# Splitting the first loads of a gated cross-attention kernel: first weight quarter on ScalarE's queue and cast by VectorE, first 400 rows of x in two pieces of 200, 24 warm-up matmuls for 31

## What is computed

```python
memory_proj = einsum('bme,de->bmd', memory, W_mem)
scores = einsum('bnd,bmd->bnm', hidden, memory_proj) / sqrt(D)
attn = softmax(scores, axis=-1)
memory_context = einsum('bnm,bmd->bnd', attn, memory_proj)
gate_input = concatenate([hidden, memory_context], axis=-1)
gate = sigmoid(einsum('bnf,df->bnd', gate_input, W_gate) + b_gate)
out = rmsnorm(hidden + gate * memory_context) * norm_w
```

## Time and profile before

| what | value |
| --- | --- |
| median of 3 runs | 294.86 us (294.81 to 295.05) |
| the profiled execution's own time | 294.93 us |
| its span, first to last instruction | 293.1 us |
| TensorE busy | 285.1 us, 97% of the span |
| VectorE busy | 175.7 us, 60% |
| ScalarE busy | 158.9 us, 54% |
| transfers | 52.19 MB, 178 GB/s over the span |

### The profile page before, as it was taken

The page is one execution under the profiler, slowest core; times in us unless marked ns, Lnnn a source line. Parts: engine busy times, 40 slices in busy tenths (PEclk is TensorE's granted clock), DMA queues, the critical chain, the costliest instruction groups (busy, mean ns, idle before and its releaser), DMA issues.

```text
span 293.1 us, 4177 instructions
## 1 busy us (share of the span) xinstructions
PE 285.1 (97%) x1671; PEld 273.7 (93%) x1671; DVE 175.7 (60%) x252; ACT 158.9 (54%) x235; POOL 4.2 (1%) x10
## 2 busy tenths in 40 slices
PE   8999999999999999999999999999999999999991
PEld 7999999898998989899898998999999999999990
DVE  2757664568656585865758562374347765476755
ACT  4648254555494645748355454435545964556632
POOL 2000000000000000000000000000000000010000
PEclk9999999999999999999999999999999999999998
DMA  6999280692948849296692411229806511623333
GB/s 209 398 401 286 101 319 0 172 351 71 323 146 217 306 121 340 76 290 229 164 358 93 127 20 58 72 72 384 180 31 225 168 48 63 134 83 94 119 131 143
DMA packets 32851, 52.19 MB, mean 178 GB/s; under 512 B 11280, under 2 KB 16144, under 8 KB 32832
## 3 DMA queue, kind: packets, MB, share of 16 engines
q1 hardware_dynamic: 32832, 51.92, 54.8%
HBM read 47.33 MB, written 4.33 MB: 176 GB/s over the span
## 4 chain that ended last, share of the span: by engine, by line
PE 92%; issue 4%; DMA 1%; ACT 1%; DVE 1%; SPq 0%; POOLq 0%; POOL 0%; ACTq 0%
PE ps L375 66%; PE ps L469 11%; PE ps L492 9%; PE ps L483 1%; DMA w_stage<-w_mem 1%; PE ps L496 1%; PE ps L503 1%; DVE acc L987 0%; DVE square_sum L964 0%; ACT gate_square L782 0%; PE ps L415 0%; PE ps L410 0%; PE ps L412 0%; POOLq L56 0%; POOL rms_late L1109 0%
## 5 line engine op out<-in xcount | busy, mean ns | idle before, releaser
L375 PE MATMUL ps<-act_hi,w_turn_hi 128*128 128x400 f32 (+2 forms) x216 | 60.4, 342 | 0.0
L375 PE MATMUL ps<-act_hi,w_turn_lo 128*128 128x400 f32 (+2 forms) x216 | 59.7, 339 | 0.0
L375 PE MATMUL ps<-act_lo,w_turn_hi 128*128 128x400 f32 (+2 forms) x216 | 59.7, 339 | 0.0
L375 PEld LDWEIGHTS ps<-act_hi,w_turn_hi 128*128 128x128 f32 x216 | 39.4, 188 | 0.9
L375 PEld LDWEIGHTS ps<-act_hi,w_turn_lo 128*128 128x128 f32 x216 | 40.0, 188 | 0.0
L375 PEld LDWEIGHTS ps<-act_lo,w_turn_hi 128*128 128x128 f32 x216 | 40.0, 188 | 0.1
L813 DVE TENSOR_TENSOR w_turn_lo<-w_stage,w_turn_hi 128x1024 fp32r<-128x1024 f32 (+2 forms) x20 | 22.3, 1116 | 24.5 <-ACT w_turn_hi L609 23.0
L813 DVE TENSOR_TENSOR cn_lo<-cn_stage,cn_hi 128x1536 fp32r<-128x1536 f32 (+1 forms) x16 | 23.7, 1484 | 5.6 <-ACT cn_hi L628 5.6
L813 DVE TENSOR_TENSOR ct_lo<-ct_stage,ct_hi 128x1444 fp32r<-128x1444 f32 x16 | 25.8, 1653 | 0.5 <-ACT ct_hi L620 0.5
L696 ACT ACTIVATE pc<-ps,row_inv 100x512 f32<-100x512 f32 x8 | 5.5, 688 | 31.5 <-PE ps L496 31.5
L609 ACT ACTIVATE w_turn_hi<-w_stage 128x1024 fp32r<-128x1024 f32 x17 | 17.9, 1053 | 7.6 <-PE ps L375 5.9
(11 more groups left out here) (147 smaller groups left out, 570.5 us busy)
## 6 DMA issues: line engine op xcount, KB each, us to landing
ct_stage<-ctxT SPq DMA_DIRECT2D x16, 722.0 KB, 8.2
cn_stage<-ctxN SPq DMA_DIRECT2D x8, 768.0 KB, 6.0
cn_stage<-ctxN SPq DMA_DIRECT2D x8, 512.0 KB, 4.1
w_stage<-w_gate_x SPq DMA_DIRECT2D x8, 512.0 KB, 6.1
w_stage<-w_gate_mc SPq DMA_DIRECT2D x8, 512.0 KB, 3.5
x_again<-xT SPq DMA_DIRECT2D x1, 2688.0 KB, 10.3
cn_stage<-ctxN SPq DMA_DIRECT2D x8, 320.0 KB
acc<-xT SPq DMA_DIRECT2D x6, 400.0 KB, 7.5
```

The lines of the kernel that those rows point to most:

```text
L375: done = nc.tensor.matmul(o, wgt, stream[h][part], start=first and wgt is wh and part == 0, stop=last and wgt is wl, skip_group_check=onto)
```

## The change

SyncE's first three transfers are now the two pieces of 200 rows of x and the second weight quarter. The first weight quarter is issued by ScalarE, as the first thing in its program, and cast by VectorE, as the first thing in VectorE's. TensorE does the six matmuls of c = 0 and 1 as twelve with 200 columns, six for each piece of x; those of c = 2 and 3 are as before. The number of warm-up matmuls goes from 31 to 24. The matmuls into the shared banks carry a flag that changes what the build tracks, not what they do.

```diff
-WARM_UP = 31
+WARM_UP = 24
...
-            sp.dma_start(acc[:, 0, 0:H], xT[0:P, 0:H]).then_inc(x_first_in, 16)
             for i in range(2):
-                cols = slice(i * C // 2, (i + 1) * C // 2)
-                sp.dma_start(w_stage[:, 0, cols], w_mem[0][:, cols]).then_inc(w_first_in[i], 16)
+                rows = slice(i * H // 2, (i + 1) * H // 2)
+                sp.dma_start(acc[:, 0, rows], xT[0:P, rows]).then_inc(x_first_in[i], 16)
+            sp.dma_start(w_stage[:, 0, C // 2:C], w_mem[0][:, C // 2:C]).then_inc(w_first_in[1], 16)
             sp.dma_start(acc[:, 0, H:R], xT[0:P, H:R]).then_inc(x_in[0], 16)
...
+                    (xh, xl) = early[0]
+                    pe.wait_ge(quarter_hi_done, 1)
+                    pe.wait_ge(first_hi_done, 1)
+                    for c, (wh, _) in pairs[0:2]:
+                        nc.tensor.matmul(left(c, 0), wh, xh, start=True, stop=False, skip_group_check=True)
+                    pe.wait_ge(first_lo_done, 1)
+                    for c, (wh, _) in pairs[0:2]:
+                        nc.tensor.matmul(left(c, 0), wh, xl, start=False, stop=False, skip_group_check=True)
+                    pe.wait_ge(first_lo_done, 2)
+                    for c, (_, wl) in pairs[0:2]:
+                        nc.tensor.matmul(left(c, 0), wl, xh, start=False, stop=False, skip_group_check=True)
...
-            act.wait_ge(x_first_in, 16)
-            nc.scalar.activation(act_hi[:, 0, 0:H], acc[:, 0, 0:H], ACT.Copy).then_inc(first_hi_done, 1)
+            act.dma_start(w_stage[:, 0, 0:C // 2], w_mem[0][:, 0:C // 2]).then_inc(w_first_in[0], 16)
             for i in range(2):
-                cols = slice(i * C // 2, (i + 1) * C // 2)
-                act.wait_ge(w_first_in[i], 16)
-                nc.scalar.activation(w_hi[0][:, cols], w_stage[:, 0, cols], ACT.Copy).then_inc(first_hi_done, 1)
+                rows = slice(i * H // 2, (i + 1) * H // 2)
+                act.wait_ge(x_first_in[i], 16)
+                nc.scalar.activation(act_hi[:, 0, rows], acc[:, 0, rows], ACT.Copy).then_inc(first_hi_done, 1)
+            act.wait_ge(w_first_in[1], 16)
+            nc.scalar.activation(w_hi[0][:, C // 2:C], w_stage[:, 0, C // 2:C], ACT.Copy).then_inc(first_hi_done, 1)
...
+            dve.wait_ge(w_first_in[0], 16)
+            nc.vector.tensor_copy(w_hi[0][:, 0:quarter], w_stage[:, 0, 0:quarter]).then_inc(quarter_hi_done, 1)
             dve.wait_ge(first_hi_done, 1)
-            minus(act_lo[:, 0, 0:H], acc[:, 0, 0:H], act_hi[:, 0, 0:H]).then_inc(first_lo_done, 1)
+            minus(act_lo[:, 0, 0:half], acc[:, 0, 0:half], act_hi[:, 0, 0:half]).then_inc(first_lo_done, 1)
```

More of the change, by code:

```diff
@@ L171, in build @@
         x_second_in, second_hi_done, second_lo_done = sem("x_second_in"), sem("second_hi_done"), sem("second_lo_done")
-        x_first_in, w_first_in = sem("x_first_in"), [sem(f"w_first_in{i}") for i in range(2)]
+        x_first_in, w_first_in = [sem(f"x_first_in{i}") for i in range(2)], [sem(f"w_first_in{i}") for i in range(2)]
+        quarter_hi_done = sem("quarter_hi_done")
         w_in = [sem(f"w_in{s}") for s in range(2)]
@@ L395, in _ @@
                 if k == 0:
[L396 to L406, removed]
+                    pairs = [(c, w_tile(0, c)) for c in range(KC)]
@@ new lines, in _, with left @@
+                    early = [(act_hi[:, 0, a:a + H // 2], act_lo[:, 0, a:a + H // 2]) for a in (0, H // 2)]
+                    def left(c, i):
+                        return bank(c, H // 2, P, i * H // 2)
+                    (xh, xl) = early[0]
[3 more added lines that the diff above has]
+                        nc.tensor.matmul(left(c, 0), wh, xh, start=True, stop=False, skip_group_check=True)
@@ new lines, in _ @@
+                    pe.wait_ge(first_lo_done, 1)
[4 more added lines that the diff above has]
+                        nc.tensor.matmul(left(c, 0), wl, xh, start=False, stop=False, skip_group_check=True)
+                    (xh, xl) = early[1]
+                    pe.wait_ge(first_hi_done, 2)
@@ new lines, in _ @@
+                    for c, (wh, _) in pairs[0:2]:
+                        nc.tensor.matmul(left(c, 1), wh, xh, start=False, stop=False, skip_group_check=True)
+                    for c, (_, wl) in pairs[0:2]:
+                        nc.tensor.matmul(left(c, 1), wl, xh, start=False, stop=False, skip_group_check=True)
+                    pe.wait_ge(first_lo_done, 3)
+                    for c, (wh, _) in pairs[0:2]:
+                        nc.tensor.matmul(left(c, 1), wh, xl, start=False, stop=False, skip_group_check=True)
@@ new lines, in _ @@
+                    (xh, xl) = halves(act_hi, act_lo, 0)[0]
+                    pe.wait_ge(first_hi_done, 3)
+                    for c, (wh, _) in pairs[2:KC]:
+                        nc.tensor.matmul(bank(c, H), wh, xh, start=True, stop=False, skip_group_check=True)
+                    for c, (wh, _) in pairs[2:KC]:
+                        nc.tensor.matmul(bank(c, H), wh, xl, start=False, stop=False, skip_group_check=True)
+                    pe.wait_ge(first_lo_done, 4)
+                    for c, (_, wl) in pairs[2:KC]:
+                        nc.tensor.matmul(bank(c, H), wl, xh, start=False, stop=False, skip_group_check=True)
@@ L409, in _ @@
                     for c, (wh, _) in pairs:
-                        nc.tensor.matmul(bank(c + 4, H), wh, xh, start=True, stop=False)
+                        nc.tensor.matmul(bank(c + 4, H), wh, xh, start=True, stop=False, skip_group_check=True)
                     for c, (_, wl) in pairs:
-                        nc.tensor.matmul(bank(c + 4, H), wl, xh, start=False, stop=False)
+                        nc.tensor.matmul(bank(c + 4, H), wl, xh, start=False, stop=False, skip_group_check=True)
                     pe.wait_ge(x_lo_done, 1)
                     for c, (wh, _) in pairs:
-                        nc.tensor.matmul(bank(c + 4, H), wh, xl, start=False, stop=False)
+                        nc.tensor.matmul(bank(c + 4, H), wh, xl, start=False, stop=False, skip_group_check=True)
                     continue
@@ L420, in _ @@
                     for c in range(KC):
-                        three([bank(c, H)], w_tile(0, KC + c), halves(act_hi, act_lo, 1)[:1], False, False)
+                        three([bank(c, H)], w_tile(0, KC + c), halves(act_hi, act_lo, 1)[:1], False, False, onto=True)
                     pe.wait_ge(x_lo_done, 2)
                     for c in range(KC):
-                        done = three([bank(c + 4, H)], w_tile(0, KC + c), halves(act_hi, act_lo, 1)[1:], False, False)
+                        done = three([bank(c + 4, H)], w_tile(0, KC + c), halves(act_hi, act_lo, 1)[1:], False, False,
+                                     onto=True)
                     done.then_inc(w_used, 1)
@@ L432, in _ @@
                         done = three([bank(c, H), bank(c + 4, H)], w_tile(k // 2 % 2, k % 2 * 4 + c),
-                                     halves(act_hi, act_lo, k), False, False)
+                                     halves(act_hi, act_lo, k), False, False, onto=True)
                 else:
@@ L437, in _ @@
                             done = three([bank(c + 4 * h, H)], w_tile(k // 2 % 2, k % 2 * 4 + c),
-                                         halves(act_hi, act_lo, k)[h:h + 1], False, True)
+                                         halves(act_hi, act_lo, k)[h:h + 1], False, True, onto=True)
                             if (h, c) != (1, KC - 1):
@@ L839, in split_ctx @@
                                                    ALU.subtract).then_inc(cn_lo_done, 1)
+            half, quarter = H // 2, C // 2
+            dve.wait_ge(w_first_in[0], 16)
+            nc.vector.tensor_copy(w_hi[0][:, 0:quarter], w_stage[:, 0, 0:quarter]).then_inc(quarter_hi_done, 1)
             dve.wait_ge(first_hi_done, 1)
-            minus(act_lo[:, 0, 0:H], acc[:, 0, 0:H], act_hi[:, 0, 0:H]).then_inc(first_lo_done, 1)
[L843 to L846, removed]
+            minus(act_lo[:, 0, 0:half], acc[:, 0, 0:half], act_hi[:, 0, 0:half]).then_inc(first_lo_done, 1)
+            dve.wait_ge(quarter_hi_done, 1)
+            minus(w_lo[0][:, 0:quarter], w_stage[:, 0, 0:quarter], w_hi[0][:, 0:quarter]).then_inc(first_lo_done, 1)
+            dve.wait_ge(first_hi_done, 2)
+            minus(act_lo[:, 0, half:H], acc[:, 0, half:H], act_hi[:, 0, half:H]).then_inc(first_lo_done, 1)
+            dve.wait_ge(first_hi_done, 3)
+            minus(w_lo[0][:, quarter:C], w_stage[:, 0, quarter:C], w_hi[0][:, quarter:C]).then_inc(first_lo_done, 1)
             dve.wait_ge(x_hi_done, 1)
```

## The result

The change measured 296.31 us in the median of 22 runs, against 294.81 us for the kernel before (22 runs, 294.35 to 295.68). The ratio is 1.0034, with a 95% interval of 1.0018 to 1.0051: it is slower, by a third of a per cent. The forecast was 294.7, within 294.2 to 295.5.

A forecast was written before the change was run, and what follows sets the result against it. TensorE, busy 97% of the span, bounds the kernel; the second weight quarter's landing decides the start. Its -0.14 us, other terms 0.0, takes 294.93 to 294.79, less 0.07 to the runs' median: 294.7 us, range 294.2 to 295.5.

The forecast's parts named there:

- the late clock: Slower rival at the kernel's start: with 24 warm-up matmuls TensorE's clock rises after the 6.1 us restart; 295.6 us, chance 0.15.
- The price: Cost of a late clock rise: nothing ahead of the 6.1 us restart, half the time until the rise after; 295.6 us.
- The first matmul: Start of TensorE's real work: first weight quarter and first piece of x arrive earlier, start 3.5 to 3.75 instead of 4.17.
- The second quarter: Transfer of the second weight quarter, on the chain at the start: lands 0.14 us earlier, the deciding term.
- The cap: If the second quarter alone came earlier, gain stops at 0.37 us, TensorE then waiting at x's right half and k = 2.
- the sum: Terms at the start together: first piece, small matmuls and warm-up 0.0 each, second quarter -0.14, from 294.93 to 294.79 us.
- The small matmuls and the table load: Before the second quarter: twelve matmuls done by 5.2, at most 5.8, and ScalarE's table load ending near 2.45; both hidden, 0.0.

The follow-up runs named there:

- the filled one: The change with 24 warm-up matmuls plus two bfloat16 matmuls behind each of the first five pairs of small matmuls; 297.17 us median, ratio 1.0056.

## Why the prediction was wrong

**The step that failed is the chance and the price of the late clock.** The mechanism was named, with its place: warm-up ending at 3.3, rise seen somewhere behind it. It was given 0.15; the change had 13 late runs of 21, and six of eight when run again. The argument against it was that "TensorE has work or warm-up for most of 0.76 to 5.2 even now". The runs show that this is no argument: with work added among the small matmuls 7 of 12 were still late, and every late profile shows TensorE at work without a break from 3.9 us on. What goes with the late runs is the length of the warm-up, here told by how far it reaches, with its starts 0.107 us apart from 0.76: to 1.6 us (8 matmuls) 4 of 4 are late; to 3.3 (24) 19 of 29 in the change, the one of 731.98 left out, and 10 of 12 in the kernel before; to 3.76 (28) 2 of 12; to 4.07 or beyond (31, 38, or 10 of 400 columns) 0 of 69 in six kernels. With a longer warm-up a hole did no harm: not one of 0.48 us inside a warm-up that reaches 4.1 (0 of 11), and not one as long in front of the first real matmul, from 4.07 to 4.55, where only the first quarter was moved (0 of 12; in its profile the full clock is on record from 4.39, inside the hole). And real matmuls that begin at 3.9 did not make up for what the warm-up lacked.

**The price.** I wrote that what is slow ahead of the second quarter is free and that behind it half of the time is lost, and said 295.6. Measured 296.57. Two terms were too small. The small matmuls were let off with "even 2.2 us from 3.6 on ends at 5.8"; at the low clock they take 0.213 us each and end at 6.60, 0.82 us behind the release. And the rise came near 9, not near the 7.6 that 295.6 amounts to.

**The first matmul.** Predicted 3.5 to 3.75, measured 3.91. The cast is 0.29 us, inside 0.21 to 0.42, but the first quarter took 2.8 us to land from ScalarE's queue, not 2.4: VectorE began at 3.56 instead of 3.1. That x's pieces on the other queue slowed it is likely and not shown. The first piece of x was late too: its cast began at 3.39, and I had written no later than 3.28. As said, it costs nothing in an early execution. The rule of the Trainium skill ("DMA: Bandwidth & Descriptors", section "Issuing engines are not separate DMA queues") agrees: the issue was 0.45 us earlier, and the landing was not (0.72 + 2.8 = 3.5 us, before 1.18 + 2.4 = 3.6).

**The second quarter.** Predicted 0.14 us sooner, measured 0.35 in the profiled execution, but the same order as before gave 0.45 in another (3.55 us against 4.00). The landing moves by itself between executions, so no part of it can be put down to the change. I had taken it for regular, from three close run times. The cap does not explain that they were close: the execution with 3.55 us kept its 0.45 us through k = 2.

**The cap.** Said to be 0.37 us behind the second quarter, with no wait at k = 2. TensorE came 0.35 ahead into k = 1 and was held 0.19 us at k = 2, since the low part of the slot was itself ready 0.22 us later (VectorE's subtraction began at 12.27, before at 12.05), which left room for 0.15. This room is no constant: in the kernel before with 24 the subtraction began at 11.80, and nothing waited. So the 0.15 us that is left of the lead comes from a landing 0.35 us sooner and a wait that was not forecast; that it is so near the 0.14 of the sum is luck.

**The small matmuls and the table load** were hidden in the early execution as said: the last small one ended at 5.68 (predicted 5.2), ahead of the 5.78 at which the next began, and the table load at 2.44 (predicted 2.45). But TensorE was to stand idle there for longer than the 0.59 us of before, and it was 0.10 us: the first matmul came later than predicted and the second quarter sooner.

**The lower group** sits at 294.77 us, against a forecast of 294.7 and a median before of 294.81. With the clock up in time, the change does nothing that can be told.

## What to carry to other kernels

An edit that shortens a warm-up changes a chance, not a duration: keep it as long as it can be hidden, and read many run times before reading any profile, because the one profiled execution can be of the good kind (here 294.84 us, below the 294.93 of the one profiled before). Price work at the start of a kernel at the lower clock as well, since what a wait hides at one level may stick out at the other. And where a stream of loads comes close behind, starting sooner gains only up to the next wait, here 0.15 us of 0.35 in one execution, and all of 0.45 in another whose loads came sooner too.

## What the runs showed of the hardware that was not expected

- The rise of the clock falls into two ranges. Each trace records from when on the full clock was granted (the column in the windows prints 1.00 ahead of that as well), and the starts of the matmuls bear this out. In ten traces this is at 3.9 to 6.6 us: 3.92 in the kernel before, 3.95 and 4.03 in the two early executions with 24, 4.35 to 6.62 in seven others, all with warm-ups that reach 4.07 us or more. In the four late ones (28, 24, 8 and the filled one) it is at 8.86 to 9.87, although TensorE worked from 3.9 on in all of them; there is none between. With 24, no rise was seen between 4.03 and 8.86, just where five of the longer warm-ups have theirs (5.27 to 6.62). This suggests that a short warm-up loses those executions whose clock would have risen there. No run shows it.
- The page "TensorE: Matmul & The Clock Gate" of the Trainium skill, section "What you observe", has the rise some 4 us into sustained matmuls, moving by half a microsecond. The early range lies around that, but is wider: 3.2 to 5.9 us behind the first matmul. The late one, 8.1 to 9.1 us behind it, is not near it where the warm-up and the real matmuls are taken as one run of work. No run here shows what makes one execution late and another not with the same program, and why five microseconds of unbroken matmuls did not bring the clock up sooner is left open.
- A transfer of 128 KB in the same place of the same queue order took 3.55 and 4.00 us in two executions.
- One run of 22 took 731.98 us. At the lower clock throughout, the real matmuls would take 0.333 for 0.183 us, 1.8 times as long, and this is 2.5 times, so that alone does not explain it. Its granted clock is on record as 1.000, where the other runs of the change have 0.995 to 0.997, and the column prints 1.00 as well while no rise has come; so a clock that never rose would fit, but no run shows it.
